# Reordering the head of a four-layer graph-attention kernel: chunk order, which engine normalises and copies, and where the mean is summed

## What is computed

```
h  = maximum(layernorm(x), 0)
Wh = h @ W                                  # 128x128
e  = leaky_relu((Wh @ a1)[:, None] + (Wh @ a2)[None, :], 0.2)
att = softmax(where(adj > 0, e, -9e15), axis=1)
x  = x + elu(att @ Wh)                      # layer 0 without elu
```

## Time and profile before

| | |
|---|---|
| median of 3 runs | 3859.01 us (3857.82 to 3859.4) |
| the profiled execution | 3859.04 us, its span 3857.2 us |
| granted clock of PE, mean | 0.999 |
| PE busy | 3817.2 us (99%) |
| DVE busy | 3582.5 us (93%) |
| ACT busy | 1241.7 us (32%) |
| POOL busy | 56.1 us (1%) |
| first matmul of the first sweep | 60.80 us from the span's start |

### The profile page before, as it was taken

One profiled execution on the slowest core, in us unless ns is written; L12 is line 12 of the kernel. 1 busy time (PEld: TensorE's weight loads), 2 busy tenths in 40 slices (PEclk: granted clock), 3 DMA queues, 4 the chain that ended last, 5 costly groups with the idle time before them and its releaser, 6 DMA issues.

```text
span 3857.2 us, 82339 instructions
## 1 busy us (share of the span) xinstructions
PE 3817.2 (99%) x34730; PEld 3790.5 (98%) x34730; DVE 3582.5 (93%) x7820; ACT 1241.7 (32%) x2603; POOL 56.1 (1%) x155
## 2 busy tenths in 40 slices
PE   7999999999999999999999999999999999999999
PEld 7999999999999999999999999999999999999999
DVE  7998989999899999999999999999997999999998
ACT  6777777777631111111133121121123000000000
POOL 3100000000000000000000000000000000000000
PEclk9999999999999999999999999999999999999999
DMA  7988888888300100000002010000000000000000
GB/s 238 306 290 298 293 295 290 290 300 293 126 17 19 18 23 18 18 21 20 15 15 67 18 20 20 18 20 20 18 18 15 16 12 18 15 15 15 15 18 9
DMA packets 223266, 344.01 MB, mean 89 GB/s; under 512 B 72496, under 2 KB 147632, under 8 KB 222896
## 3 DMA queue, kind: packets, MB, share of 16 engines
q1 hardware_dynamic: 221168, 338.48, 27.9%
q10 hardware_dynamic: 1728, 0.27, 0.0%
HBM read 305.70 MB, written 21.20 MB: 85 GB/s over the span
## 4 chain that ended last, share of the span: by engine, by line
PE 95%; ACT 2%; DVE 2%; DMA 1%; issue 1%; DVEq 0%; SPq 0%; ACTq 0%; POOL 0%
PE acc L1297 92%; PE ps_wh L1315 1%; ACT vals L1506 1%; DVE q L812 1%; PE ps_pack L1203 1%; ACT adj_pairs L1411 0%; DMA adj_int<-in_adj_dram 0%; DMA vals<-in_x_dram 0%; DVE mask L775 0%; PE acc L1279 0%; ACT xnew L1518 0%; PE ps_bc L1255 0%; PE acc L1233 0%; PE ps_pack L1210 0%; PE ps_wh L1233 0%
## 5 line engine op out<-in xcount | busy, mean ns | idle before, releaser
L1297 PE MATMUL acc<-vals,q 128*128 128x129 f32 (+1 forms) x32576 | 3666.8, 275 | 4.0 <-DVE q L812 3.7
L1297 PEld LDWEIGHTS acc<-vals,q 128*128 128x128 f32 x32576 | 3648.8, 192 | 17.7 <-issue 9.4
L812 DVE SCALAR_TENSOR_TENSOR q<-rrow,R,mask 128x512 f32<-128x512 f32 x3968 | 2822.9, 748 | 148.3 <-PE acc L1297 20.2
L1411 ACT ACTIVATE adj_pairs<-adj_int,threshold 128x1024 uint8<-128x1024 int32 x512 | 585.9, 1148 | 214.2 <-PE ps_pack L1203 130.6
L775 DVE TENSOR_SCALAR mask<-bits 128x512 uint16<-128x512 uint16 x2048 | 438.8, 291 | 7.0 <-DMA rrow<-rows 4.1
L1518 ACT ACTIVATE xnew<-acc,rec 128x128 f32<-128x128 f32 x244 | 69.4, 366 | 843.2 <-DVE rec L850 748.2
L1525 ACT ACTIVATE e<-xnew 128x512 f32<-128x512 f32 x47 | 29.7, 632 | 407.1 <-DVE xnew L881 318.8
L1538 ACT ACTIVATE e<-xnew,nm,rs 128x128 f32<-128x128 f32 x193 | 79.8, 485 | 219.5 <-DVE nm L647 219.5
L1591 ACT ACTIVATE wh<-ps_wh 128x512 f32<-128x512 f32 x48 | 28.7, 599 | 338.7 <-PE ps_wh L1315 337.8
L1533 ACT ACTIVATE sd<-ve 128x4 f32<-128x4 f32 (+1 forms) x49 | 9.9, 203 | 365.2 <-DVE ve L628 365.2
L881 DVE SCALAR_TENSOR_TENSOR xnew<-mean,none,xnew 128x128 f32<-128x128 f32 x188 | 65.2, 347 | 48.4 <-ACT xnew L1518 48.4
(11 more groups left out here) (241 smaller groups left out, 837.1 us busy)
## 6 DMA issues: line engine op xcount, KB each, us to landing
adj_int<-in_adj_dram SPq DMA_DIRECT2D x512, 512.0 KB, 4.9
rrow<-rows SPq DMA_DIRECT2D x60, 256.0 KB, 3.2
x_between_layers<-xnew SPq DMA_DIRECT2D x32, 256.0 KB, 3.7
xin<-x_between_layers SPq DMA_DIRECT2D x32, 256.0 KB, 2.8
xin<-in_x_dram SPq DMA_DIRECT2D x16, 256.0 KB, 5.4
wh_of_layer<-wh SPq DMA_DIRECT2D x1, 4096.0 KB, 16.8
x_of_layer<-xnew SPq DMA_DIRECT2D x16, 256.0 KB, 2.3
xin<-x_of_layer SPq DMA_DIRECT2D x16, 256.0 KB, 2.8
```

The costliest lines, as they stand in the source:

```text
L812: nc.vector.scalar_tensor_tensor(q[:, j % RING, :], row, column(R_, t), mask[:, c % 2, j, :], ALU.max, ALU.mult).then_inc(q_ready, 1)
L1297: last = nc.tensor.matmul(to, q[:, j % RING, b * P:(b + 1) * P], vals[:, t, 0:width(g.layer)], start=first, stop=(t == KT - 1 or g.two and ...
L1411: nc.scalar.activation(adj_bytes[:, n % BIN_RING // 2, :, n % 2], adj_int[:, n % ADJ_RING, :], ACT.Sign, bias=threshold[:, 0:1], accum_out ...
```

## The change

- Chunks in order on DVE: statistics and normal rows of chunk c, then chunk c+1. DVE normalises 8 tiles of a chunk, POOL the other 8.
- Only layer 0's weights are turned ahead of the first group; those of layers 1 to 3 are turned by PE behind group 2, their score columns behind group 4.
- ACT's first piece of `adj` comes ahead of the first group, the others in a table of its own; 11 instead of 12 pieces stand ahead of the sweep (`BEGUN`). ACT's ReLU leaves out the sum per row.
- DVE copies `wh` and `s` of groups 11 to 15 (`FIRST_WH_BY_DVE`), ACT those of 0 to 10. The bits of the first chunk are unpacked between two of these copies.
- PE spreads `s1` (the row scores) in the head, behind group 10, before the maximum is known; the row's argument is added by DVE straight from PSUM and its exponential taken by ACT. Layer 3 has the same order.
- The mean of layer 0: behind its 48 `vals`, POOL adds the 16 groups of `wh` (15 additions of 128x512). PE sums the result over partitions with four matmuls behind tile 60 of group 0, and DVE makes the mean in group 1.
- In the redo loop ahead of layer 3, ACT takes the ELU ahead of a row copy, and DVE unpacks layer 3's first bits inside the loop.

```diff
-BEGUN = 12
+BEGUN = 11
+FIRST_WH_BY_DVE = 11
...
# POOL
             for c in range(CHUNKS):
                 pool.wait_ge(norm_scales, c + 1)
-                for n in range((c + 1) * JC - BLOCKS, (c + 1) * JC):
+                for n in range(c * JC + JC // 2, (c + 1) * JC):
...
                         if t % SUB == SUB - 1:
                             last.then_inc(vals_ready, 1)
+                    total = nc.gpsimd.tensor_tensor(sums_0[:, :, :], wh[:, 0:BLOCKS, :], wh[:, BLOCKS:2 * BLOCKS, :], ALU.add)
+                    for v in range(2, GROUPS):
+                        total.then_inc(wh_added, 1)
+                        pool.wait_ge(wh_added, v - 1)
+                        total = nc.gpsimd.tensor_tensor(sums_0[:, :, :], sums_0[:, :, :],
+                                                        wh[:, v * BLOCKS:(v + 1) * BLOCKS, :], ALU.add)
+                    total.then_inc(h_mean_ready, 1)
...
# DVE
-            first_statistics(0)
             for c in range(CHUNKS):
-                if c + 1 < CHUNKS:
-                    first_statistics(c + 1)
+                first_statistics(c)
                 first_normal(c)
+            for v in range(FIRST_WH_BY_DVE, GROUPS):
+                first_wh(v)
+                if v == FIRST_WH_BY_DVE:
+                    unpack(Rows(0, 0), 0)
...
             def start_of_layer(st):
-                if st.layer == 0:
-                    unpack(Rows(st.layer, 0), 0)
                 greatest(st)
-                total_of_h(st.layer)
-                shifts(st)
-                if st.layer == 3:
-                    unpack(Rows(st.layer, 0), 0)
+                if st.layer > 0:
+                    total_of_h(st.layer)
+                column_shifts(st)
+                row_argument(st)
                 lift(st)
+                row_shifts(st)
...
# PE
+                if v == 2:
+                    turn_other_weights()
+                if v == 4:
+                    other_score_columns()
-                if v == QP:
+                if v == QP + 1:
                     pack(0, 0)
-                keep_busy(LEFT_IN_HEAD.get(v, 0), ps_bc)
+                if v == 10:
+                    pe.wait_ge(wa_copied, 2)
+                    spread_s1(WHOLE[0])
+                if v in LEFT_IN_HEAD:
+                    pe.wait_ge(bits_ready, 1)
+                    keep_busy(LEFT_IN_HEAD[v], ps_pack)
...
+                    if g.layer == 0 and g.value == 0 and t == 60:
+                        mean_row(0)
...
# ACT
-                                     ACT.Relu, accum_out=h_sum[:, v:v + 1]).then_inc(hT_ready[0], 1)
+                                     ACT.Relu).then_inc(hT_ready[0], 1)
...
+            binary(0, 0)
+            pieces = {0: (1,), 1: (2,), 2: (3,), 5: (4,), 6: (5,), 7: (6,), 8: (7,), 12: (8,), 14: (9,), 15: (10,)}
             for v in range(GROUPS):
                 first_hT(v)
-                if v > 0:
+                if 0 < v <= FIRST_WH_BY_DVE:
                     first_wh(v - 1)
-                if v % BLOCKS == BLOCKS - 1 and v // BLOCKS + 2 < CHUNKS:
-                    first_deviations(v // BLOCKS + 2)
-                if v < QP or v % 2 == 0:
-                    binary(0, v if v < QP else (v + QP) // 2)
+                if v in (2, 5, 8):
+                    first_deviations((v + 1) // 3)
...
```

More of the change, by code:

```diff
@@ L675, in first_normal @@
                 dve.wait_ge(norm_scales, c + 1)
[L676 removed]
+                for n in range(c * JC, c * JC + JC // 2):
                     last = nc.vector.tensor_scalar(x_rows_0[:, n, :], x_rows_0[:, n, :], rs_0[:, n:n + 1],
@@ L688, in greatest @@
             def greatest(st):
-                dve.wait_ge(wh_ready[st.layer], st.tiles.stop // BLOCKS)
+                dve.wait_ge(wh_ready[st.layer], FIRST_WH_BY_DVE if st.layer == 0 else st.tiles.stop // BLOCKS)
+                if st.layer == 0:
+                    dve.wait_ge(wh_by_dve, GROUPS - FIRST_WH_BY_DVE)
                 if st.n > 0:
@@ L756, in make_mean @@
                 dve.wait_ge(mean_done, mean_index[k] + 1)
+                if k == 0:
+                    steps.did(nc.vector.tensor_scalar(mean[:, :], ps_mean, 1.0 / N, None, ALU.mult))
+                    return
                 steps.did(nc.vector.tensor_copy(mean[:, :], ps_mean))
@@ L996, in trip_of_unit @@
                     op, amount = (ALU.logical_shift_left, 6 - b) if b <= 6 else (ALU.logical_shift_right, 1)
-                    last = nc.vector.tensor_scalar(mask_words[:, 0, 0:1, b, :], bits[:, u.value // BLOCKS, tile, :],
+                    last = nc.vector.tensor_scalar(words_of_unit[:, :, b, :], bits[:, u.value // BLOCKS, tile, :],
                                                    amount, ONES, op, ALU.bitwise_and)
@@ L1096, in between @@
                         smallest({20: 0, 24: 1, 40: 2}[t])
+                    if g.layer == 0 and g.value == 1 and t == 3:
+                        make_mean(0)
                     if g.last:
@@ L1105, in sweep @@
                     chunk(g, c, between)
-                    if g.value == 0 and c == 0 and not g.two:
+                    if g.value == 0 and c == 0 and g.layer == 3:
                         make_mean(g.layer)
@@ L1235, in first_project, with spread, spread_s1 @@
                 last.then_inc(wh_done[0], 1)
+            def spread(columns, to):
+                for b in range(columns.shape[1]):
+                    last = nc.tensor.matmul(to[:, b * P:(b + 1) * P], columns[:, b:b + 1].broadcast_to([P, P]),
+                                            ident[:, :], start=True, stop=True)
+                return last
+            def spread_s1(st):
+                pe.wait_ge(wh_ready[st.layer], 1)
+                spread(s[:, 0, 0:BLOCKS], ps_bc).then_inc(row_done, 1)
             first_transposes(0)
@@ L1467, in _ @@
+                if v == 6:
+                    act.wait_ge(wa_done, 2)
+                    nc.scalar.activation(w_sb[:, 1:LAYERS, F:F + 2],
+                                         ps_bc[:, 3 * P:3 * P + 6].rearrange("p (k c) -> p k c", k=LAYERS - 1), ACT.Copy)\
+                        .then_inc(wa_copied, 1)
+                for n in pieces.get(v, ()):
+                    binary(0, n)
+                if v == QP + 3:
                     words(0, 0)
-            first_wh(GROUPS - 1)
             def exponentials(st):
```

141 lines of the change are left out of this document (99 added, 42 removed).

## The result

The changed kernel takes **3870.28 us** (median of 7 runs, 3868.84 to 3872.67) where the one before takes 3857.73 us beside it: ratio 1.0032, 95% interval 1.0022 to 1.0042. Forecast were 3868.6 us and a range of 3855 to 3876. The medians differ by 12.6 us, the spans of the two profiled executions by 10.4 (3867.6 against 3857.2).

What follows compares the result with a forecast made beforehand. The prediction took PE as the bound, busy 95% of the span, with ACT's chain in the head. Head -4.4, layer 3 -1.2 and mean +15.2 gave +9.6 us on 3859.04: 3868.6 us, range 3855 to 3876.

Steps and rivals of the forecast that it cites:

- The head: Ahead of the first sweep: chunks in order and less ACT work bring the first matmul to 56.4 us, -4.4 us.
- Layer 3 and the redo loop: Ahead of layer 3: an earlier ReLU and root, and a changed start, together -1.2 us.
- The term of -0.3: Layer 3's start: DVE waits for a spread of 1.99 us that overlaps the maximum; -0.3 us, bounds 0 and -1.
- The mean: Behind tile 60 of the first sweep: PE waits for POOL's 15 additions, plus matmuls and half-pace restart; +15.2 us.
- turns with `q`: During POOL's additions: each takes its turn behind a DVE `q`, part of the reason for taking 1.5 us per addition.
- 8 tiles ahead: During PE's stop for the mean: DVE runs 8 tiles ahead and then stops too, so nothing is made up.
- the pieces of `adj`: On ACT and SP: they move with PE and cost nothing, covered by PE's 0.90 us per tile.
- the late piece: Packing behind tile 4: ACT's piece 15 lands just in time; if not, PE waits about 0.5 us.
- Additions at 1.2 undisturbed: Rival on the mean: POOL's additions run undisturbed at 1.2 us, stop 7.8 us, total 3864.1 us; chance 0.27.
- The sum in time: Rival on the mean: additions at 0.70 us, below 0.86 us each, end 0.3 us late; 3854.6 us, chance 0.12.
- the head gains in full: Rival: ACT never waits in the head, -7.5 us, and the sum is in time; about 3851 us, chance 0.07.
- 2.1 us or more: Rival on the mean: each addition takes at least this long, stop 21.3 us, 3877.6 us and up; chance 0.08.

Runs made afterwards that it cites:

- a quarter on POOL: Against the kernel with ScalarE's sums: POOL normalises 4 of a chunk's 16 rows and DVE 12, as before the change; 3857.77 us, ratio 1.0000.
- without fillers: 12 idle-filling PE matmuls left out of the head: from the kernel with ScalarE's sums, 3855.06 us; from a later version with ACT's last root moved, 3850.93 us.
- one addition: Changed kernel with all but one of POOL's fifteen additions left out, so 14 of 16 groups are missing in the mean; 3856.49 us, ratio 0.9996.
- ScalarE's sums: Changed kernel with the mean's sums taken by ACT's ReLU per row, as before the change, and no POOL additions; 3857.06 us, ratio 0.9997.
- The later landing: Against the kernel with ScalarE's sums: SP waits for the transposed row to land behind piece 20, not piece 12; 3854.89 us, ratio 0.9991.
- Moving the consumer away: Changed kernel with all fifteen additions, but PE takes the mean's row 12 tiles into the next group; 3866.79 us, ratio 1.0020.

## Why the prediction was right, and where not

*The head* (-4.4, came -4.04). The order was right: ACT held by DVE's chain of chunks, then PE's own list. DVE waited 0.63 us for ACT's root of chunk 0, since ACT's table load stood ahead of it (11.76 to 13.04), and the normal rows came at 14.68 and not 14.25; this cost nothing behind, for DVE went on with chunk 1's scales at 22.54 where I had 22.45. The small errors came later: two rounds of DVE took 7.94 and 7.95 us and not 7.70, so PE's last stretch began at 40.07 and not 39.5, and it took 12.46 us (to 52.53) and not 12.2. From the maximum to the first matmul it was 3.32 us where I had 3.63, which gave 0.3 back. DVE's copy from PSUM took 0.69 where I took 0.70. That DVE's chain and PE's own list set the end is shown by the runs with a quarter on POOL (+2.5) and without fillers (-1.16).

*Layer 3 and the redo loop* (-1.2, came -2.5). From the redo loop's first spread to layer 3's maximum it is 16.79 us (2925.80 to 2942.59) and was 17.65, -0.86 where I had -0.9. The rest is the start: maximum to first matmul 3.55 us, was 5.17 (2931.25 to 2936.42). I had read the spread's 1.99 us as its price; it ran at half pace then, behind a wait of PE of 1.55 us for `h_mean`, and takes 1.15 now, behind one of 0.75. It overlaps the maximum, and DVE waits only 0.21 us for it. The term of -0.3 came as -1.6, mis-sized by 1.3 us. This is read from the traces; no run undid it alone.

*The mean* (+15.2). The stop is 12.21 us, forecast 12.3; the matmuls and the restart 2.58, forecast 2.9. The additions took 1.51 us at the median, and 1.60 from start to start, forecast 1.5; their chain is 22.9 us, forecast 22.5. My reason, turns with `q`, was a part of it only: alone an addition takes 1.27, and 0.24 are the turns. The value came out right because I took a middle between far bounds, not because I knew its parts: that is luck. One step was wrong and cost nothing: DVE didn't run 8 tiles ahead and stop. It was busy without a gap until 129.6 us, past the end of the additions at 128.4.

*What wasn't there.* I costed the pieces of `adj` at nothing and named PE's 0.90 per tile as their cover. The sweep that starts earlier overtakes SP's round trip for the row, and PE waits at two packings, 0.77 us in all in the changed kernel, 2.09 with one addition and 1.47 with ScalarE's sums. With what each wait costs besides, the way to the mean's place is longer by 1.26, 2.42 and 1.80. The later landing proved the cause of the long wait, at the packing at 92 us; the short one, behind tile 4, is the late piece that the prediction named and took for in time. Two misses, +1.26 here and -1.3 in layer 3, cancel, and so do +0.4 in the head and -0.4 in the mean; that the sum came so near is luck in both. It was 9.6 against 10.4 in the spans, and the rest is 0.2 in the sweeps between and the 0.6 at the end. By the medians it was 9.6 against 12.6.

*The rivals.* Additions at 1.2 undisturbed would have been 3864.1: alone they take 1.27, near it, but they don't run alone. Even at 1.36 a piece, 1.27 and the gap of 0.09, they would end at 105.5 + 20.4 = 125.9 us, 9.6 us after PE asks (116.25). The sum in time fell by its own condition, below 0.86 us each. That the head gains in full fell with DVE's chain, and 2.1 us or more with the row of additions. The Trainium skill (GPSIMD Engine Reference, section 3.1, Elementwise) was of more use than I made of it: its 4497 ns for 2048 columns is met here, since 1.27 at 512 and 0.73 at 256 columns give 2.11 ns per column and 0.19 us besides, 4.51 us at 2048, an estimate. Dividing its figure by four loses the fixed part. Its other page (SBUF — State Buffer, Who interferes with whom) speaks of a lock for the whole of an instruction. That both grow, `q` to 1.66 us and the additions to 1.51, agrees; the size doesn't. One `q` and one addition by themselves take 0.75 + 1.27 = 2.02 us, and together a pair takes 1.60 to 1.66, so in part they run at once. The page also says that one-input operations of DVE can hold the shared ports in some forms, which the unpacking at 5.6 us agrees with; the prediction left that out.

## What to carry to other kernels

Work that moves to an idle engine has its price at two places: its own chain against the moment it is needed, and the engine that slows down beside it, here DVE. Moving the consumer away cured only the first, and a third of the loss. Two microseconds won ahead of a long stretch are won only if the streams inside that stretch have them too: look for every place where a queue waits for a round trip. And a sum that a write gives along, as ACT's ReLU does here, cost nothing measurable on an engine that waits anyway.

## What the runs showed of the hardware

- A GpSimd addition of two 128x512 fp32 tiles: 1.27 us alone, 1.31 beside DVE's unpacking, 1.51 beside `q`. Beside it DVE's `q` goes from 0.75 to 1.66 us and the unpacking, eight instructions, from 1.7 to 5.6. DVE pays far more than GpSimd.
- In the head PE's granted clock fell to 1.2 GHz after PE had waited, at 40 to 46 us in the profiled executions of four kernels, at 33 to 40 us in four others, and not at all in the kernel before, the changed kernel and the two without fillers. In the run with one addition it moved the first matmul by 1.34 us; in the run with ScalarE's sums, where PE still had to wait for rows, by nothing (56.69). All eight had the fillers behind group 12, which come too late for that stretch; one profiled execution of each kernel doesn't show how often it falls.
